# Multiplying the attended heads with wo as f32r products of halves in a one-core attention and expert kernel

## What is computed

```python
h = _layernorm(x, axis=-1) * (1 + ca) + sa
q, k, v = (_heads(h @ w.T) for w in (wq, wk, wv))        # 16 heads of 64
phi_q, phi_k = _phi(q, omega), _phi(k, omega)            # exp(proj - norm) / 8
kv_cumsum = jnp.cumsum(jnp.einsum('bhnm,bhnd->bhnmd', phi_k, v), axis=2)
k_cumsum = jnp.cumsum(phi_k, axis=2)
out = jnp.einsum('bhnm,bhnmd->bhnd', phi_q, kv_cumsum)
out = out / (jnp.einsum('bhnm,bhnm->bhn', phi_q, k_cumsum) + 1e-06)[..., None]
attn = out.transpose(0, 2, 1, 3).reshape(b, n, H * D) @ wo.T + bo
x = x + ga * attn
h = _layernorm(x, axis=-1) * (1 + cb) + sb
x = x + gb * experts(h)                                  # top 2 of 8, with a capacity
```

## Time and profile before

| | |
|---|---|
| median of 3 runs | 726.92 us |
| the profiled execution | 727.18 us |
| its span, first to last instruction | 725.1 us |
| mean granted TensorE clock in it | 0.992 |
| busy: PE, PE's weight loads, DVE, ACT, POOL | 697.4, 604.1, 536.0, 387.6, 335.6 us |

### The profile page before, as it was taken

One profiled execution on the slowest core, in us unless ns is written; L12 is line 12 of the kernel. 1 busy time (PEld: TensorE's weight loads), 2 busy tenths in 40 slices (PEclk: granted clock), 3 DMA queues, 4 the chain that ended last, 5 costly groups with the idle time before them and its releaser, 6 DMA issues. The chain is left out here.

```text
span 725.1 us, 27349 instructions
## 1 busy us (share of the span) xinstructions
PE 697.4 (96%) x11452; PEld 604.1 (83%) x11452; DVE 536.0 (74%) x1685; ACT 387.6 (53%) x740; POOL 335.6 (46%) x625
## 2 busy tenths in 40 slices
PE   8999999999999999999999999999999789999956
PEld 8788888888888888888888888888887779999942
DVE  6687888878878887888878878888775456565416
ACT  5755566665656665666656566665552144544310
POOL 3002545555544445454545554545447306556550
PEclk9999999999999999999999999999999999999989
DMA  9974000000000000000000000000000154553128
GB/s 252 362 268 178 11 9 11 10 9 11 14 15 10 11 10 11 10 10 11 9 11 11 14 14 9 11 11 11 10 11 14 49 177 130 168 173 113 51 82 304
DMA packets 32705, 47.25 MB, mean 65 GB/s; under 512 B 4132, under 2 KB 20168, under 8 KB 32584
## 3 DMA queue, kind: packets, MB, share of 16 engines
q1 hardware_dynamic: 23296, 32.62, 13.4%
q0 software_dynamic: 4096, 8.42, 3.6%
q10 hardware_dynamic: 5192, 4.47, 1.9%
HBM read 22.21 MB, written 23.36 MB: 63 GB/s over the span
## 5 line engine op out<-in xcount | busy, mean ns | idle before, releaser
L1297 POOL DMA_INDIRECT y_rows<-y_sb,row_id x64 | 62.8, 982 | 66.0 <-DVE y_sb L1442 49.9
L1108 POOL DMA_INDIRECT dispatched<-h_cur,slot x64 | 67.3, 1051 | 17.8 <-issue 16.1
L1376 ACT ACTIVATE hidden<-bank,b_col 128x512 f32<-128x512 f32 x64 | 43.3, 689 | 58.2 <-PE bank L1348 57.8
L632 ACT ACTIVATE phi_k<-expo_k 128x1024 f32<-128x1024 f32 x32 | 33.9, 1058 | 74.5 <-DVE expo_k L768 70.7
L648 ACT COPY v_sb<-bank 128x512 f32<-128x512 f32 x64 | 37.6, 587 | 62.1 <-PE bank L279 58.7
L527 PEld LDWEIGHTS bank<-woT,attT 128*128 128x128 f32 x512 | 61.9, 192 | 3.2 <-ACT attT L738 0.6
L859 DVE TENSOR_TENSOR scores<-bank,within 128x512 f32<-128x512 f32 x64 | 41.2, 686 | 31.2 <-PE bank L310 31.2
L527 PE MATMUL bank<-woT,attT 128*128 128x128 f32 x512 | 62.4, 275 | 0.4 <-ACT attT L738 0.4
L1317 PE MATMUL bank<-w_sb,hidden 128*128 128x128 f32 x512 | 59.7, 275 | 0.8 <-issue 0.8
L137 POOL TENSOR_TENSOR rs<-var,power 128x1 f32<-128x1 f32 x64 | 37.1, 579 | 49.8 <-DVE var L132 49.5
L1317 PEld LDWEIGHTS bank<-w_sb,hidden 128*128 128x128 f32 x512 | 58.3, 192 | 1.2 <-issue 1.2
(11 more groups left out here) (243 smaller groups left out, 2037.9 us busy)
## 6 DMA issues: line engine op xcount, KB each, us to landing
dispatched<-blank SPq DMA_DIRECT2D x16, 524.0 KB, 3.1
region<-dispatched SPq DMA_DIRECT2D x30, 262.0 KB, 2.9
y_rows<-blank SPq DMA_DIRECT2D x8, 512.0 KB, 3.9
w_nat<-in_L_ffn_w_dram SPq DMA_DIRECT2D x8, 256.0 KB, 3.7
y_got<-y_rows SPq DMA_DIRECT2D x8, 256.0 KB, 6.8
y_got<-y_rows ACTq DMA_DIRECT2D x8, 256.0 KB, 7.4
out_dram<-x_sb SPq DMA_DIRECT2D x8, 256.0 KB, 3.7
w_sb<-in_L_ffn_w_dram ACTq DMA_DIRECT2D x6, 256.0 KB, 2.8
```

The costliest lines, as they stand in the source:

```text
L1108: pool.indirect_dma_start(out=dispatched[:, :], in_=h2_cur[par][:], in_offset=None, out_offset=bass.IndirectOffsetOnAxis(ap=slot[par][:, k ...
L1297: pool.indirect_dma_start(out=y_rows[:, :], out_offset=bass.IndirectOffsetOnAxis(ap=row_id[par][:, t:t + 1].bitcast(U32), axis=0), in_=y_s ...
L1376: act.activation(hidden[par][:, k, :], psum[2 + k][:], ACT.Gelu, bias=b1_col[:, bass.ds(e * KH + k, 1)]).then_inc(sem(f"hid{k}_out"), 1)
```

## The change

Both factors are kept as two f32r tiles, a high part and what is left of it, and `add_heads` does for each of the 8 pairs of heads three f32r matmuls of 128 columns: high by high, high by low, low by high. The low by low product is left out. ACT's two copies per step now write `attT_hi` (semaphores `attT0_hi`, `attT1_hi`). DVE forms `attT_lo` from the banks and `attT_hi` in two subtractions of 128x512 per step (`heads_low`), which stand between `choose` and `state_add(1)`, and it is these that now give `attT0_out` and `attT1_out`. The low part of the transposed `wo` is made once, by two DVE subtractions at the end of its opening, which now give `woT_ready`. `sgn` and `mag` move into the space of a weight that is not needed any more.

```diff
-                attT = tsb("attT", [P, NP, P])
+                attT_hi = tsb("attT_hi", [P, NP, P], F32R)
+                attT_lo = tsb("attT_lo", [P, NP, P], F32R)
...
+                            o = psum[BANK["wo"]][:, 0:D]
                             for t in range(NP):
-                                mm = pe.matmul(psum[BANK["wo"]][:, 0:D], attT[:, t, :], woT[:, t, :], start=(t == 0), stop=(t == NP - 1))
+                                pe.matmul(o, attT_hi[:, t, :], woT_hi[:, t, :], start=(t == 0), stop=False)
+                                pe.matmul(o, attT_hi[:, t, :], woT_lo[:, t, :], start=False, stop=False)
+                                mm = pe.matmul(o, attT_lo[:, t, :], woT_hi[:, t, :], start=False, stop=(t == NP - 1))
                             mm.then_inc(sem("wo_in"), 1)
...
                                 act.wait_ge(sem("woT_filled"), half + 1)
-                                act.copy(woT[:, half * 4:half * 4 + 4, :].rearrange("p j d -> p (j d)"), psum[4 + half][:]).then_inc(sem("woT_ready"), 1)
+                                act.copy(woT_hi[:, half * 4:half * 4 + 4, :].rearrange("p j d -> p (j d)"), psum[4 + half][:]).then_inc(sem("woT_hi_done"), 1)
...
                                     act.wait_ge(sem(f"attT{half}_in"), c)
-                                    act.copy(attT[:, half * 4:half * 4 + 4, :].rearrange("p a b -> p (a b)"),
-                                             psum[BANK[f"attT{half}"]][:]).then_inc(sem(f"attT{half}_out"), 1)
+                                    act.wait_ge(sem("wo_in"), c - 1)
+                                    act.copy(attT_hi[:, half * 4:half * 4 + 4, :].rearrange("p a b -> p (a b)"),
+                                             psum[BANK[f"attT{half}"]][:]).then_inc(sem(f"attT{half}_hi"), 1)
...
                             first_norm(dve, 2, 0)
+                            for half in range(2):
+                                tiles = slice(half * 4, half * 4 + 4)
+                                dve.wait_ge(sem("woT_hi_done"), half + 1)
+                                dve.tensor_tensor(woT_lo[:, tiles, :].rearrange("p j d -> p (j d)"), psum[4 + half][:],
+                                                  woT_hi[:, tiles, :].rearrange("p j d -> p (j d)").bitcast(F32),
+                                                  ALU.subtract).then_inc(sem("woT_ready"), 1)
...
+                            def heads_low():
+
+                                for half in range(2):
+                                    pairs = slice(half * 4, half * 4 + 4)
+                                    dve.wait_ge(sem(f"attT{half}_hi"), c)
+                                    dve.tensor_tensor(attT_lo[:, pairs, :].rearrange("p a b -> p (a b)"), psum[BANK[f"attT{half}"]][:],
+                                                      attT_hi[:, pairs, :].rearrange("p a b -> p (a b)").bitcast(F32),
+                                                      ALU.subtract).then_inc(sem(f"attT{half}_out"), 1)
...
                             if last and c != NCH:
                                 choose()
+                            if tail:
+                                heads_low()
                             if back:
                                 state_add(1)
```

More of the change, by code:

```diff
@@ L81, in build @@
         wT_lo = {k: sb(f"w{k}_lo", [P, HD], F32R) for k in ("q", "k", "v", "pq", "pk")}
-        woT = sb("woT", [P, NP, D])
+        woT_hi = sb("woT_hi", [P, NP, D], F32R)
+        woT_lo = sb("woT_lo", [P, NP, D], F32R)
         wg_sb = sb("wg_sb", [P, E])
@@ L182, in attention @@
                 h2T = tsb("h2T", [P, P])
-                sgn = tsb("sgn", [P, B * D])
-                mag = tsb("mag", [P, B * D])
                 lg_now = tsb("lg_now", [P, E])
@@ L200, in attention @@
                 wo_nat = tsb("wo_nat", [P, HD])
+                sgn, mag = (w_nat["k"][:, i * 4:i * 4 + 4, :].rearrange("p j d -> p (j d)") for i in range(2))
                 om_blk = tsb("om_blk", [P, P])
@@ L810, in bound_gate @@
                                 dve.tensor_copy(b1_col[:], psum[4][:, 0:E * KH])
-                            dve.tensor_scalar(sgn[:], g, 0.0, -0.5, ALU.is_ge, ALU.add).then_inc(sem("d_chain"), 1)
+                            dve.tensor_scalar(sgn, g, 0.0, -0.5, ALU.is_ge, ALU.add).then_inc(sem("d_chain"), 1)
                             dve.wait_ge(sem("d_chain"), 3 * m + 3)
-                            dve.scalar_tensor_tensor(out=mag[:], in0=g, scalar=4.0, in1=sgn[:], op0=ALU.mult, op1=ALU.mult).then_inc(sem("d_chain"), 1)
+                            dve.scalar_tensor_tensor(out=mag, in0=g, scalar=4.0, in1=sgn, op0=ALU.mult, op1=ALU.mult).then_inc(sem("d_chain"), 1)
                             dve.wait_ge(sem("d_chain"), 3 * m + 4)
-                            dve.scalar_tensor_tensor(out=g, in0=mag[:], scalar=0.5, in1=sgn[:], op0=ALU.max, op1=ALU.mult).then_inc(sem("d_chain"), 1)
+                            dve.scalar_tensor_tensor(out=g, in0=mag, scalar=0.5, in1=sgn, op0=ALU.max, op1=ALU.mult).then_inc(sem("d_chain"), 1)
                             dve.wait_ge(sem("d_chain"), 3 * m + 5)
```

## The result

The changed kernel takes **780.14 us** (median of 4 runs, 778.80 to 781.45) against 727.02 us for the kernel before on the same chip: a ratio of 1.0732, with a 95% interval of 1.0706 to 1.0758. The forecast was 781 us. The profiled execution took 781.33 us, its span is 779.3 us and its mean granted clock 0.984 (0.992 before).

A forecast was written before the change was run, and what follows sets the result against it. PE, busy 96% of the span, was taken as the bound; 28.5 (product) + 24.5 (rank wait) + 0.9 (closing) + 0.4 (opening) = 54.3 us over the median of 726.92 gave 781 us, range 757 to 798.

The forecast's parts named there:

- The product, +28.5 us: PE's product with wo: 24 f32r matmuls at 0.112 us replace 16 fp32 passes, +0.89 us a step over 32 steps.
- The wait at the rank, +24.5 us: PE's rank matmuls wait for DVE's subtractions to release attT1: 0.86 us in 27 steps, 0.43 in three.
- DVE does not give it back: DVE still waits for PE's scores at the mask, so the same 0.86 us is lost again in the next step.
- The closing, +0.9: In the closing, DVE's subtractions come between ACT's copies and the product, which starts at 560.27 instead of 559.40: +0.9 us.
- The opening, +0.4: In the opening, bias_T on PE waits for DVE's first wo subtraction, 1.9 us later, mostly absorbed: +0.4 us.
- the squares of its first half let PE go on about 0.4 later: Opening: q's projection ends about 31.2; PE, which had waited for ACT's squares at 30.83, resumes about 0.4 us later.
- The stream that binds (740): Product rival: columns, not loads, set the pace, 0.058 us a matmul, -12.6 us, total 740 us; chance 0.04.
- the load that hides in part (761): Product rival: loads partly hidden, 0.085 us a matmul, +8 us, total 761 us; chance 0.04.
- fp32's double pace (867): Product rival: f32r at 128 columns no faster than fp32, 0.223 us a matmul, +114 us, total 867 us; chance 0.06.
- the stall that is not there (757): Rank rival: DVE reaches choose 0.86 us earlier, so PE does not stall; total 757 us; chance 0.03.
- the faster one: Product rival: matmuls under 0.040 us apart pay for the stall; about 719 us at 0.030; chance 0.01.

The follow-up runs named there:

- The run with 48 loads: Changed kernel with each of the 24 product matmuls cut into two of 64 columns: 967.25 us, ratio 1.3295 to the kernel before.
- the one with 16: Changed kernel with attT_hi meeting both halves of wo in one 256-column matmul, DVE adding the bank's halves: 749.07 us, ratio 1.0289 to the kernel before.

## Why the prediction was right, and where it was off

The two large terms were right in their mechanism. That the total came within 1 us is in part luck: the wait at the rank was some 3 us smaller than forecast, and the opening some 2 us larger.

- **The product, +28.5 us.** Right in mechanism and size: 0.112 us a matmul, and 0.92 a step for a forecast of 0.89. The run with 48 loads and the one with 16 show that the load sets it and not the columns. The row that gave the 0.112 did not show that: the first two fp32 passes of the product before stand 0.108 us apart in most steps, at the place where two f32r matmuls stand 0.06 apart because the load hides. So an fp32 pass takes nearly that long by its columns alone, and that its pace and the price of an f32r load agree was luck; the spacing of the loads in the earlier trace rows was the better argument. The Trainium skill (TensorE: Matmul & The Clock Gate, section LDWEIGHTS) has the time of a load go with the columns that are loaded, P / 1.2, an estimate of 107 ns for 128; the 0.111 to 0.112 us of these runs agree at the full clock. At the half clock of the run with 48 loads it was 0.21. The 81 ns that the Trainium skill has for a pair at 128 columns (TensorE: Matmul & The Clock Gate, section Back-to-back issue gap), against which the prediction argued from the fp32 rows, did not come: 0.112 was measured.
- **The wait at the rank, +24.5 us.** Right in mechanism, and most of the time goes when the rank moves; too large by some 3 us. A wait costs 0.74 and not 0.86, mainly because the rank started 0.05 us after the second subtraction had ended (332.12 to 332.17), where 0.14 was reckoned, and there are 28 of them and not 30.
- **DVE does not give it back.** Right, and this was the step on which most hung: DVE's idle time ahead of the mask is 0.98 us in step 16, as before, and 33.1 us in all (31.2 before), so DVE has not fallen behind PE, and a delay of PE is not made up.
- **The closing, +0.9.** Measured 0.8 of a wait.
- **The opening, +0.4.** Wrong, by its size. The step that failed is "the squares of its first half let PE go on about 0.4 later": between the q projection and the k projection PE still has eight transposes (line 297, 0.8 us), and k's first matmul follows them without a wait for the squares. At the full clock the q projection comes 1.6 us later than before, measured from the `pk` ahead of it, and the slack ahead of k's takes up only 0.9 of that; 0.7 us is lost. On top, in some executions the clock went to half behind the wait, another 1.6 us, which the prediction had nowhere.
- **The rivals.** The stream that binds (740), the load that hides in part (761) and fp32's double pace (867) fall with the distance of 0.112; the stall that is not there (757) with the 28 waits of 0.74; the faster one would have needed matmuls 0.040 us apart.

## What to carry to other kernels

A matmul pays for its weight load when it has few columns: here an f32r matmul of 64 or of 128 columns cost 0.11 us, so three products of halves at that width cost three loads, and putting two of them into one matmul with a shared stationary operand won back 0.76 of the 0.92 us a step. When a bank is handed on by another engine than before, look at who takes the bank next, and not only at who reads the result: some 21 of the 54 us lay at a use that has nothing to do with the product.

## What the runs showed of the hardware

- A dense row of f32r matmuls of 64 columns lost the full clock in the middle of a product (granted 1.00, then 0.56 and 0.50, mean of the execution 0.875), although PE never stood still; the same loads with 128 columns, 24 in a row, kept it.
- A wait of 1.74 us in the opening was followed by 3.3 us at a granted 0.52 in one execution of the changed kernel, and by none in another with the same wait; of six kept executions with it, four show a low clock there.
- Loads hid behind a long neighbour and not behind short ones: behind a 512-column matmul the product's second f32r matmul came 0.06 us after its first, behind the 16-column ones of the rank 0.14.
- Where its load was hidden, an f32r matmul made way for the next after 0.03 us with 64 columns and 0.06 with 128; an fp32 pass of 128 columns at the same place took 0.108.
